# One product of 24 columns instead of three of 8 for the maxima in a graph kernel's message pass

## The reference

```python
Q = relu(x @ query_kernel + query_bias)[row];  K = relu(x @ key_kernel + key_bias)[col];  V = (x @ kernel)[col]
att = sum(Qh * Kh, axis=-1)                       # 8 scores an edge
smax = segment_max(att, row);  sexp = exp(att - smax[row]);  alpha = sexp / segment_sum(sexp, row)[row]
out = segment_sum(Vh * alpha[:, :, None], row) + bias
x = layernorm(x + out)
```

## Time and profile before

| | |
|---|---|
| median of 3 runs (lowest to highest) | 12965.54 us (12961.75 to 12969.74) |
| the profiled execution | 12931.55 us, span 12929.9 us |
| busy in the whole span | PE 8780.0, DVE 8062.3, ACT 4075.8, POOL 3319.8 us |
| message pass, 4782 to 6225 us | PE 1420.38, DVE 924.05, ACT 864.76, POOL 878.00 us |

### The profile page before, as it was taken

One profiled execution on the slowest core, in us unless ns is written; L12 is line 12 of the kernel. 1 busy time (PEld: TensorE's weight loads), 2 busy tenths in 40 slices (PEclk: granted clock), 3 DMA queues, 4 the chain that ended last, 5 costly groups with the idle time before them and its releaser, 6 DMA issues. The chain is left out here.

```text
span 12929.9 us, 326466 instructions
## 1 busy us (share of the span) xinstructions
PE 8780.0 (68%) x98373; PEld 7278.6 (56%) x98374; DVE 8062.3 (62%) x17566; ACT 4075.8 (32%) x8798; POOL 3319.8 (26%) x3879
## 2 busy tenths in 40 slices
PE   6134558867886459999544444444479996959996
PEld 5132226647775449999433333333334994639996
DVE  7587777779997666666522222222257887778887
ACT  0130001113332125555211111111157884633332
POOL 0000001100000016666355555555500221321110
PEclk9999999999997569999766666666689998979997
DMA  1100000004442113333122222222266440000000
GB/s 34 11 0 5 4 5 11 11 8 153 163 162 92 33 54 123 122 122 123 53 76 75 74 76 77 76 75 76 76 208 209 146 146 23 5 4 3 3 3 11
DMA packets 529166, 882.81 MB, mean 68 GB/s; under 512 B 133643, under 2 KB 221286, under 8 KB 529115
## 3 DMA queue, kind: packets, MB, share of 16 engines
q1 hardware_dynamic: 437099, 758.43, 17.4%
q0 software_dynamic: 62592, 122.00, 3.8%
q10 hardware_dynamic: 29424, 1.83, 0.1%
HBM read 735.41 MB, written 146.54 MB: 68 GB/s over the span
## 5 line engine op out<-in xcount | busy, mean ns | idle before, releaser
L2402 POOL DMA_INDIRECT e_row<-r_table,e_idx x1760 | 1669.0, 948 | 1519.8 <-DVE e_idx L1797 961.8
L1797 DVE COPY e_idx<-gather_d 128x4 uint32 (+1 forms) x444 | 78.6, 177 | 2354.5 <-ACT e_s L2467 1559.0
L2438 PE MATMUL e_tps<-ident_b,e_oh 128*128 128x128 bf16 x1760 | 261.8, 304 | 1595.3 <-DVE e_oh L2419 1335.7
L2343 POOL TENSOR_TENSOR acc<-acc,m_sum 128x544 f32<-128x544 f32 (+1 forms) x637 | 811.2, 1273 | 1289.8 <-ACT m_sum L2310 1008.8
L2438 PEld LDWEIGHTS e_tps<-ident_b,e_oh 128*128 128x128 bf16 x1760 | 151.9, 128 | 1695.2 <-DVE e_oh L2419 1385.1
L2447 PE MATMUL e_ps<-ident,e_row 128*128 128x128 f32 x3520 | 988.0, 370 | 83.8 <-issue 80.7
L2467 ACT COPY e_s<-e_ps 128x512 f32<-128x512 f32 x440 | 257.8, 586 | 1847.2 <-remote 1367.5
L2447 PEld LDWEIGHTS e_ps<-ident,e_row 128*128 128x128 f32 x3520 | 705.0, 248 | 115.4 <-issue 112.2
L2450 PE MATMUL e_ps<-e_ohT,p_part 128*128 128x128 bf16 x5280 | 712.2, 254 | 51.2 <-issue 51.2
L2273 PE MATMUL m_sps<-m_msg,m_oh 128*128 128x136 f32 x5096 | 722.5, 286 | 0.0
L2208 DVE TENSOR_TENSOR m_msg<-m_vps,m_msg 128x512 f32<-128x512 f32 x637 | 440.7, 692 | 371.3 <-PE m_vps L2249 296.7
(11 more groups left out here) (535 smaller groups left out, 22002.7 us busy)
## 6 DMA issues: line engine op xcount, KB each, us to landing
s_rows<-bucket_rows SPq DMA_DIRECT2D x148, 768.0 KB, 4.0
m_rows<-bucket_rows SPq DMA_DIRECT2D x148, 768.0 KB, 4.0
e_edges<-e_s SPq DMA_DIRECT2D x440, 256.0 KB
f_e<-e_edges SPq DMA_DIRECT2D x440, 256.0 KB, 3.0
o_e<-e_edges SPq DMA_DIRECT2D x440, 256.0 KB, 2.8
s_rows<-bucket_rows SPq DMA_DIRECT2D x49, 1024.0 KB, 5.3
m_rows<-bucket_rows SPq DMA_DIRECT2D x49, 1024.0 KB, 5.4
e_row<-r_table,e_idx POOLq DMA_INDIRECT x1760
```

What stands on the lines that cost most here:

```text
L2343: nc.gpsimd.tensor_tensor(at, at, sums[x][:, 0:n * M], ALU.add).then_inc(added, 1)
L2402: nc.gpsimd.indirect_dma_start(row[u][:, j * D:(j + 1) * D], None, table, bass.IndirectOffsetOnAxis(ap=idx[u][:, j:j + 1], axis=0)).then_i ...
L2438: last = nc.tensor.transpose(tps[u % 2][:, j * P:(j + 1) * P], oh[u][:, j * P:(j + 1) * P], k["ident_b"][:, :])
```

## The change

`most(q)` issues one product a tile, with the 24 columns of the three parts as its moving operand, instead of three that add up in PSUM. `m_mps` grows from 4 × 8 to 4 × 24 fp32 columns. VectorE's `lessen(q)` first adds the three parts with a reduce out of PSUM into a new tile `m_top` in SBUF (4 × 8 columns), waits for that, and subtracts `m_top` from the scores. The wait that frees `m_mps` for TensorE is still the one on the subtraction.

```diff
-        vb, mover = sb("m_vb", TW, BF16), sb("m_over", OV * MW, BF16)
-        mps, ops = ps("m_mps", G * H), ps("m_ops", GE, BF16)
+        vb, mover, top = sb("m_vb", TW, BF16), sb("m_over", OV * MW, BF16), sb("m_top", G * H)
+        mps, ops = ps("m_mps", G * MW), ps("m_ops", GE, BF16)
...
                         dve.wait_ge(m_made[x], X.before(w, q) + 1)
                         dve.wait_ge(exped[x], X.before(w, q) + 1)
+                        nc.vector.tensor_reduce(top[:, :].rearrange("p (j h) -> p j h", h=H), mps[:, :].rearrange("p (j c h) -> p j h c", c=3, h=H),
+                                                AX, ALU.add).then_inc(summed, 1)
+                        dve.wait_ge(summed, w * NQ + (q + 1))
                         nc.vector.tensor_tensor(diff[x][:, :].rearrange("p (j h) -> p j h", h=H),
                                                 att[:, bass.ds(half * W, W)].rearrange("p (j q h) -> p q j h", j=G, h=H)[:, q],
-                                                mps[:, :].rearrange("p (j h) -> p j h", h=H), ALU.subtract).then_inc(less[x], 1)
+                                                top[:, :].rearrange("p (j h) -> p j h", h=H), ALU.subtract).then_inc(less[x], 1)
...
                             table = mparts[:, t * MW:(t + 1) * MW] if t < s.NB else mover[:, (t - s.NB) * MW:(t - s.NB + 1) * MW]
-                            for c in range(3):
-                                last = nc.tensor.matmul(mps[:, j * H:(j + 1) * H], oht[r][:, j * P:(j + 1) * P], table[:, c * H:(c + 1) * H],
-                                                        start=(c == 0), stop=(c == 2))
+                            last = nc.tensor.matmul(mps[:, j * MW:(j + 1) * MW], oht[r][:, j * P:(j + 1) * P], table, start=True, stop=True)
                         last.then_inc(m_made[x], 1)
```

More of the change, by code:

```diff
@@ L2137, in phase_messages @@
         lists_in = sem("m_lists_in", own=True)
-        lists_free, go, vb_set, turned, added, add_go = (sem("m_" + x) for x in ("lists_free", "go", "vb_set", "turned", "added", "add_go"))
+        lists_free, go, vb_set, turned, summed, added, add_go = (sem("m_" + x) for x in ("lists_free", "go", "vb_set", "turned", "summed", "added", "add_go"))
         oht_made = [sem(f"m_oht_made{r}") for r in range(O.size)]
```

## The result

The changed kernel takes 13334.36 us (13327.92 to 13343.14, four runs), the kernel before 12965.87 us in the same series (the three runs of its table and one more): ratio 1.0287, 95% interval [1.0274, 1.0299], +368 us. The prediction said 13305 us, with a narrow range of 13290 to 13370 for its own mechanism inside the wide one of 13050 to 13550. The profiled execution took 13327.92 us, 396 us more than the one before.

What follows compares the result with a forecast made beforehand. TensorE looked like the message pass's bound before; after, a GpSimd-add, subtraction and evacuation loop: 49 × 6.9 = 340 us onto 12931.55 gives 13271, plus 34 to the median: 13305 us, range 13050 to 13550 (own 13290 to 13370).

Steps and rivals of the forecast that it cites:

- lock: Message pass: subtraction with two SBUF inputs waits out GpSimd's add, again each quad; 2.91 us a quad, chance 0.58.
- 0.04 to 0.17 us ahead of the add: Message pass, VectorE: lead over GpSimd's add that an op with two SBUF inputs needs to escape being held.
- The step: Message pass, locked quad: GpSimd's add ends at E, the next starts at E + 1.57, ends at E + 2.91.
- The total, +340 us: Message pass: a window of 36.4 us against 29.47, 6.9 us more in each of 49 windows.
- 0.48 after the cast: ScalarE in a locked quad: evacuation starts 0.48 us after the cast; GpSimd's next add 0.87 after that.
- Reduce and signal, 0.28 us: VectorE, each quad: reduce of 96 elements 0.25 us, wait for its signal 0.03; bounds 0.19 and 0.40 us.
- TensorE's saving: Message pass: eight of twelve products dropped, 0.26 us a quad; worth nothing under lock, 166 us in full (rival, chance 0.03).
- upper bound of 0.058 us: TensorE: dearest a 24-column product could be, from the transposes' 128 columns, 0.23 / 4 us.
- No lock: Rival: subtraction not held up by GpSimd's add; window some 0.3 us shorter, 12953 us; chance 0.10.
- The slip: Rival: some subtractions start ahead of GpSimd's add; 2.4 us a quad, window 32.3 us, 13104 us; chance 0.19.
- The one-hot op was not caught: Rival: GpSimd's add also holds VectorE's one-hot op; 3.5 us a quad, 13536 us; chance 0.05.
- TensorE's clock: Rival: in the message pass TensorE, partly idle, gets 1.2 instead of 2.4 GHz; 3.8 us a quad, near 13950 us; chance 0.05.

Runs made afterwards that it cites:

- experiment 1: Changed kernel with m_top in PSUM, so the subtraction reads one SBUF and one PSUM input: 13045.53 us, ratio 0.9993 to the kernel before.
- experiment 2: Kernel before, twelve products kept, but m_mps copied to SBUF and the subtraction reading the copy: 13325.33 us, ratio 1.0207 to the kernel before.
- experiment 5: Changed kernel with ScalarE's reads of block numbers moved ahead of the exp: 12460.15 us, ratio 1.0287 to the kernel before.
- run 7: Changed kernel, m_top in SBUF, with VectorE's subtraction for the next quad ahead of the one-hot op: 12076.58 us, ratio 0.9968 to the kernel before.
- run 8: Changed kernel with m_top in PSUM and VectorE's subtraction ahead of the one-hot op: 12985.88 us, ratio 0.9943 to the kernel before.
- experiment 6: Changed kernel with m_top in PSUM, but twelve products of 8 columns, each into its own columns: 12147.75 us, ratio 1.0024 to the kernel before.
- experiment 10: Changed kernel with m_top in PSUM, subtraction ahead of the one-hot op, ScalarE's reads early: 12043.04 us, ratio 0.9933 to the kernel before.

## Why the prediction was right

**The place and the mechanism.** Slower, by a lock between one subtraction and one add, is what the trace shows and what experiments 1, 2 and 3 show from three sides: the second input moved to PSUM (loss gone), the second input in SBUF alone (most of the loss, +266 of +368 us), the add shortened (step shortened by as much). The inference from the earlier trace rows was the deciding one: a subtraction with one PSUM input goes through an add, the last stage's weighting with two SBUF inputs doesn't. One detail did not carry over: the prediction let an instruction in only if it starts 0.04 to 0.17 us ahead of the add, by a one-hot op that was caught 0.03 us ahead. A subtraction gets in from 0.02 us ahead.

**The step.** All terms of E + 0.08, + 0.22, + 0.70, + 1.57 were read as predicted, and the step of 2.91 us too.

**The total, +340 us.** The stage grew by 370. The term that was mis-sized is the evacuation, "0.48 after the cast": taken from a quad without ScalarE's reads, used for all eight. In three of them it is 0.7, so the eight steps take 23.95 us instead of 8 × 2.91 = 23.28. Experiment 5 shows it: without the reads in that place the window is 36.39. The base, 34 us from the profiled execution to the median, was about right, since the medians differ by 368 us: 12965.5 + 340 = 13305, and 34 us of reads give 13339, with 13334 measured. The profiled execution of after has 20 us more in an untouched stage (columns of `f_z`, 451.6 to 471.9 us), which the medians don't show; it stays unexplained.

**Reduce and signal, 0.28 us.** The reduce was 0.25 as worked out from the earlier trace rows. The signal was not 0.03 as in the earlier trace rows: from the reduce's start to the subtraction's are 0.39 us (5509.84 to 5510.23), so 0.14 lies between the recorded end and the next start. It isn't in the 2.91, and made the lock firmer: the subtraction is 0.17 us behind the add, not 0.05. Here the prediction had luck. ScalarE's reads, which it left out, put an add 0.2 us later, and in one quad of a window only the longer signal still keeps the subtraction behind it, by about 0.02 us. With a signal of 0.03 that subtraction would start some 0.09 us ahead of the add and get in, as in experiment 2. By the steps there (2.04 and 2.17 us in place of 2.91 and 3.11) a window would be 1.8 us shorter and the kernel near 13246 us: an estimate, and outside the narrow range of 13290 to 13370. Two terms that were missed cancelled there.

**TensorE's saving.** The 0.26 us a quad was too much: the prediction took a product of 24 columns as cheap as one of 8 (0.0325 us), and it takes 0.05 us (runs 7 and 8), so the saving is 0.20 us and TensorE's own pace 1.98 us. Its upper bound of 0.058 us was read from a recorded span; by the distance of starts (5507.37 to 5507.56 in run 8) the four transposes take 0.19 us, 0.048 each. In the changed kernel the saving is worth nothing, as said, since the transposes wait 285 us for ScalarE's cast. Without the lock it would be worth 41 us (0.84 × 49, experiment 6), not 166.

**The rivals.** No lock would have given a window some 0.3 us shorter, 12953 us; experiment 1 is that case, with 0.25 us and a ratio of 0.9993. The slip occurs in experiment 2, and in the changed kernel in one window. The one-hot op was not caught in the locked steps (0.48 us at 5509.44), and its mean fell from 677 to 548 ns. TensorE's clock didn't fall: 1.00 in the stage, though its products fill 1420 of 1825 us.

## What to carry to other kernels

Before an operand of VectorE moves from PSUM to SBUF, look at what GpSimd does at that moment: a short instruction with two SBUF inputs can be held for a whole add, and if what GpSimd waits for hangs on that instruction, the two lock in turn. Keep one input in PSUM, or order VectorE's queue so that the short instruction starts a few tenths before GpSimd's. And when a step is costed from one repetition of a loop, look through the others for what they have in their queues besides.

## What the runs showed of the hardware that was not expected

- For the subtraction the order of start is sharp. One that starts 0.02 us behind the add of a quad is held for all of it (1.37 us), and at 0.00 to 0.01 us some are held and some are not; the 51 of the changed kernel that start 0.02 to 0.09 us ahead of one take 0.19 us, and the add then up to 1.38 us instead of 1.34.
- For the one-hot op the edge lies elsewhere. In the kernel before, 48 start 0.02 to 0.04 us ahead of an add by the trace and are held all the same (1.64 to 1.66 us), as in the earlier trace rows; in run 7 those that start 0.05 us or more ahead go through (0.49 us). Whether the recorded starts or the instructions differ is not shown.
- A held instruction ends soon after the add, the later the more elements it has: 0.05 us for 32 fp32 elements, 0.28 us for the one-hot op with 1024.
- The one-hot op (one bf16 SBUF input, 1024 elements) holds GpSimd's add in turn: up to 1.63 us instead of 1.34 (run 7).
- A signal from a 0.25 us reduce to the subtraction behind it cost 0.14 us beyond the recorded end (0.13 to 0.24 over a run), behind the copy of 0.19 us as much, where a 0.47 us instruction showed 0.03. Why they differ stays open.
- A register read on ScalarE made a locked step 0.2 to 0.3 us longer (3.11 and 3.19 against 2.91 us), and cost nothing where ScalarE's queue was not the bound (experiment 10).
- Four products of 24 columns took 0.20 us with their weight loads, twelve of 8 columns 0.39: 0.05 and 0.033 us each.
- In the profiled execution of the changed kernel the granted clock was recorded near 0.5 in the first 2900 us, where before it was 1.00. Yet TensorE was busy 738 and 737 us from 2000 to 2900 us, and a load at the start of the next stage begins at 2941.9 and 2941.7 us. The record of the clock alone was no evidence of lost time.
